# A patch's last 48 rows and the bias: one f32 product against two f16 products on stacked rows

## The reference

```
patches = X cut into 8 x 8 patches of 28 x 28 x 3           # 64 patches of 2352 values, batch 128
tokens  = concat(cls, patches @ W.T + b) * pos_embed        # 65 tokens of 128 values
h = tokens + lstm(layernorm(tokens))                        # 65 steps, state of 128
logits = layernorm(h) @ router_w.T + router_b               # 16 experts, the best 2 of them
out = h + sum over the 2 experts: gate * (gelu(ln @ w1.T + b1) @ w2.T + b2)
```

## Time and profile before

| | |
|---|---|
| time, median of 3 runs | 673.26 us (672.86 to 674.25) |
| the profiled execution | 674.92 us, of it a span of 673.1 us |
| busy, share of the span | PE 92%, PEld 87%, DVE 84%, ACT 73%, POOL 61% |
| mean granted TensorE clock | 0.986 |
| DMA | 141.67 MB, mean 210 GB/s |

### The profile page before, as it was taken

How to read it: one execution, slowest core, us unless ns; L and a number is a source line. 1 busy time by engine, 2 the same in 40 slices (tenths; PEclk the granted TensorE clock), 3 DMA queues, 4 the chain that set the end, 5 groups by cost and what they waited for, 6 DMA issues and landing times.

```text
span 673.1 us, 24553 instructions
## 1 busy us (share of the span) xinstructions
PE 619.0 (92%) x7952; PEld 587.0 (87%) x7952; DVE 562.3 (84%) x1797; ACT 489.7 (73%) x1259; POOL 411.9 (61%) x446
## 2 busy tenths in 40 slices
PE   4899999999999999999998967999999999999970
PEld 4899999999999999999998856788888898888860
DVE  3887888888888888988989878997787887889896
ACT  3687877666677666665665457778888888999883
POOL 0233333477677776667656677777777666666571
PEclk9999999999999999999999989999999999999995
DMA  8987887688888888877876113445554445555675
GB/s 308 384 285 272 267 274 251 235 265 273 267 277 273 265 274 255 247 238 260 263 245 205 52 54 100 112 130 169 165 142 115 120 114 158 156 174 160 188 224 201
DMA packets 71895, 141.67 MB, mean 210 GB/s; under 512 B 13078, under 2 KB 55650, under 8 KB 63838
## 3 DMA queue, kind: packets, MB, share of 16 engines
q1 hardware_dynamic: 62128, 121.69, 58.1%
q0 software_dynamic: 9280, 17.21, 7.3%
q10 hardware_dynamic: 366, 1.21, 0.5%
HBM read 116.35 MB, written 25.66 MB: 211 GB/s over the span
## 4 chain that ended last, share of the span: by engine, by line
PE 57%; DVE 8%; issue 6%; DMA 5%; POOL 3%; ACT 1%; SPq 0%; POOLq 0%; ACTq 0%; DVEq 0%
PE pair L1281 22%; PE pair L1436 11%; PE pair L1454 11%; PE pair L1327 4%; DMA patches<-sent 4%; PE pair L1291 3%; PE pair L1410 2%; DVE patches L1099 2%; PE pair L1296 1%; POOL back L1259 1%; PE pair L1382 1%; DMA field<-back 1%; POOL sent L1235 1%; PE pair L1353 1%; PE pair L1316 1%
## 5 line engine op out<-in xcount | busy, mean ns | idle before, releaser
L1259 POOL DMA_INDIRECT back<-patches x160 | 156.7, 979 | 69.0 <-issue 54.7
L1281 PE MATMUL pair<-field,patches 128*128 128x128 f32 (+1 forms) x1408 | 173.7, 280 | 9.2 <-DMA patches<-in_x 9.2
L1235 POOL DMA_INDIRECT sent<-pay,slot_own x130 | 148.9, 1146 | 40.0 <-issue 37.0
L1281 PEld LDWEIGHTS pair<-field,patches 128*128 128x128 f32 (+1 forms) x1408 | 164.4, 194 | 9.5 <-issue 8.0
L680 ACT ACTIVATE pair<-pair,b1s 128x256 f32<-128x256 f32 x320 | 123.1, 448 | 29.0 <-PE pair L1436 28.3
L605 ACT ACTIVATE gate<-pair,lbias 128x128 f32<-128x128 f32 x260 | 74.1, 367 | 81.4 <-PE pair L1296 79.5
L1247 POOL TENSOR_TENSOR rstd<-veps,cst 128x2 f32<-128x2 f32 (+1 forms) x68 | 57.4, 844 | 94.7 <-DVE veps L800 94.2
L1436 PE MATMUL pair<-patches,ex_hi 128*128 128x256 f16 x640 | 109.8, 274 | 6.0 <-DVE patches L1099 3.7
L1454 PE MATMUL pair<-ex_hi,patches 128*128 x1280 | 111.4, 219 | 2.9 <-DVE patches L1099 1.5
L1099 DVE TENSOR_TENSOR patches<-pair,patches 128x1024 f16<-128x1024 f32 x80 | 97.2, 1215 | 1.7 <-ACT patches L689 1.7
L1281 PE MATMUL pair<-field 128*128 128x128 f16 x1536 | 96.1, 219 | 0.0
(11 more groups left out here) (150 smaller groups left out, 1232.2 us busy)
## 6 DMA issues: line engine op xcount, KB each, us to landing
patches<-in_x SPq DMA_DIRECT2D x62, 1152.0 KB
patches<-sent SPq DMA_DIRECT2D x80, 130.0 KB
field<-in_we SPq DMA_DIRECT2D x64, 128.0 KB
field<-back SPq DMA_DIRECT2D x10, 768.0 KB, 5.2
patches<-in_b SPq DMA_DIRECT2D x80, 64.0 KB
field<-in_pos SPq DMA_DIRECT2D x65, 64.0 KB
out_tower<-h SPq DMA_DIRECT2D x10, 384.0 KB
back<-patches POOLq DMA_INDIRECT x160
```

What stands on the lines that cost most here:

```text
L1235: pool.indirect_dma_start(sent, bass.IndirectOffsetOnAxis(ap=slot_own[:, g % 4, choice, col:col + 1], axis=0), pay[:, t % NP, :], None, bo ...
L1259: pool.indirect_dma_start(back, bass.IndirectOffsetOnAxis(ap=dsti[j % NO][:, k:k + 1], axis=0), yo[j % NO][:, k, :], None, bounds_check=2 ...
L1281: last = pe.matmul(bank_of, l, w_, start=(c == KS and k == 0), stop=(c == KS - 1 and k == 2))
```

## The change: what it does

The rest of a patch moves from the f32 part to the f16 part. Its 48 rows and the row of ones are now loaded twice into one chunk of 128 partitions: rows 0 to 47 and again 64 to 111, with ones in the rows between and behind. The weights of that chunk hold the rounded weights in rows 0 to 63 and their f16 remainders in rows 64 to 127, the bias in row 48 of each half and zeros behind it. One f16 matmul over 128 rows then gives rounded patch times rounded weights plus rounded patch times remainder, and a second one over 64 rows gives patch remainder times rounded weights. The f16 chunks are now the last 8 and the rest, and the f32 chunks the first 10, so the f32 part has one chunk less and the f16 part two matmuls more. ACT's second half of the split grows from 4 chunks to 5, DVE's `xlo` from 8 to 9. SP issues one more load of 48 rows for each patch. On ACT's queue the rest of the weights comes in six small loads, ahead of the 8 chunks that are split. The buffer for position rows has 3 places and not 4.

```diff
-NPOS = 4
+NPOS = 3
 def load_patches(t):
...
-    sp.dma_start(xraw[q][0:KREST, KC, :], x[bass.ds(row + KC * P, KREST), :]
-                 ).then_inc(x_in[q], 16)
+    for first in (0, STACK):
+        sp.dma_start(xraw[q][first:first + KREST, KC, :], x[bass.ds(row + KC * P, KREST), :]
+                     ).then_inc(x_in[q], 16)
...
-act.dma_start(ws[:, 0:KC - KS, :], w[:, KS:KC, :]).then_inc(w_in, 16)
-act.dma_start(ws[0:KBIAS + 1, KC - KS, :], w_rest).then_inc(w_in, 16)
-act.dma_start(ws_raw, w[:, 0:KS, :]).then_inc(ws_in, 16)
+act.dma_start(ws[:, :, :], w[:, 0:NF, :]).then_inc(w_in, 16)
+for first in (0, STACK):
+    act.dma_start(ws_raw[first:first + KREST, KS, :], w_rest[0:KREST, :]).then_inc(ws_in, 16)
+    act.dma_start(ws_raw[first + KREST:first + KREST + 1, KS, :], w_rest[KBIAS:KBIAS + 1, :]
+                  ).then_inc(ws_in, 16)
+    act.dma_start(ws_raw[first + KREST + 1:first + STACK, KS, :], w_rest[KREST:KBIAS - 1, :]
+                  ).then_inc(ws_in, 16)
+act.dma_start(ws_raw[:, 0:KS, :], w[:, NF:KC, :]).then_inc(ws_in, 16)
...
-    split(t, KS // 2, KS).then_inc(hi_done, 1)
+    split(t, KS // 2, KS + 1).then_inc(hi_done, 1)
...
+dve.scalar_tensor_tensor(whi[STACK:P, KS, :], ws_raw[STACK:P, KS, :], W_SCALE, whi[STACK:P, KS, :], ALU.mult,
+                         ALU.subtract)
...
-    dve.tensor_tensor(xlo[r][:, :, :], xraw[q][:, 0:KS, :], xhi[r][:, :, :],
+    dve.tensor_tensor(xlo[r][:, :, :], xraw[q][:, NF:KC + 1, :], xhi[r][:, :, :],
                       ALU.subtract).then_inc(lo_done, 1)
...
 for c in range(a, b):
-    if c < KS:
-        parts = [(l[r][:, c, :], w_[:, c, :]) for l, w_ in ((xhi, whi), (xhi, wlo), (xlo, whi))]
+    s = c - NF
+    if c < NF:
+        parts = [(xraw[q][:, c, :], ws[:, c, :])]
+    elif c < KC:
+        parts = [(l[r][:, s, :], w_[:, s, :]) for l, w_ in ((xhi, whi), (xhi, wlo), (xlo, whi))]
     else:
-        rows = slice(0, P if c < KC else KBIAS + 1)
-        parts = [(xraw[q][rows, c, :], ws[rows, c - KS, :])]
+        parts = [(xhi[r][:, s, :], whi[:, s, :]), (xlo[r][0:STACK, s, :], whi[0:STACK, s, :])]
...
-        project(k, KS, KC + 1)
+        project(k, 0, NF)
...
-    project(t, 0, KS).then_inc(tok_done, 1)
+    project(t, NF, KC + 1).then_inc(tok_done, 1)
```

More of the change, by code:

```diff
@@ L33 @@
 KS = 8
+NF = KC - KS
+STACK = 64
 E, FF = 16, 512
@@ L125, in piece_of_field, with chunks_of_field @@
             return field[:, spent[0] - words:spent[0]]
[L127 to L133, removed]
+        def chunks_of_field(n):
+            return piece_of_field(n * P // 2).bitcast(F16).rearrange("p (a b) -> p a b", a=n)
+        ws = piece_of_field(NF * HID).rearrange("p (a b) -> p a b", b=HID)
+        xhi = [chunks_of_field(KS + 1) for i in range(2)]
+        xlo = [chunks_of_field(KS + 1) for i in range(2)]
+        whi, wlo = chunks_of_field(KS + 1), chunks_of_field(KS)
         posr = piece_of_field(NPOS * HID).rearrange("p (a b) -> p a b", b=HID)
@@ L145, in tower @@
         late = ex_lo[:, E // 2:E, :, :].rearrange("p e m f -> p (e m f)").bitcast(F32)
-        ws_raw = late[:, 0:KS * HID].rearrange("p (a b) -> p a b", a=KS)
-        wih = late[:, KS * HID:(KS + 4) * HID].rearrange("p (a b) -> p a b", a=4)
-        whh = late[:, (KS + 4) * HID:(KS + 8) * HID].rearrange("p (a b) -> p a b", a=4)
+        ws_raw = late[:, 0:(KS + 1) * HID].rearrange("p (a b) -> p a b", a=KS + 1)
+        wih = late[:, (KS + 1) * HID:(KS + 5) * HID].rearrange("p (a b) -> p a b", a=4)
+        whh = late[:, (KS + 5) * HID:(KS + 9) * HID].rearrange("p (a b) -> p a b", a=4)
         b1s = sb("b1s", [P, E * FC])
@@ L315, in tower @@
         N_FIRST, N_WEIGHTS, N_CONST = 2, 4, 3
+        N_STACKED = 7
         R_MASK, R = 12, 16
@@ L449, in load_patches @@
                 if t <= 2:
[L450 removed]
+                    sp.dma_start(xraw[q][:, 0:NF, :], here[:, 0:NF, :]).then_inc(x_in[q], 16)
                 else:
                     sp.dma_start(xraw[q][:, 0:KC, :], here).then_inc(x_in[q], 16)
[L453 to L454 removed]
+                for first in (0, STACK):
+                    sp.dma_start(xraw[q][first:first + KREST, KC, :], x[bass.ds(row + KC * P, KREST), :]
+                                 ).then_inc(x_in[q], 16)
                 if t <= 2:
[L456 removed]
+                    sp.dma_start(xraw[q][:, NF:KC, :], here[:, NF:KC, :]).then_inc(x_head[q], 16)
             sp.wait_ge(ones_in, 1)
@@ L568, in _ @@
             expert_of = act.alloc_register("expert_of")
-            act.dma_start(ws[:, 0:KC - KS, :], w[:, KS:KC, :]).then_inc(w_in, 16)
-            act.dma_start(ws[0:KBIAS + 1, KC - KS, :], w_rest).then_inc(w_in, 16)
-            act.dma_start(ws_raw, w[:, 0:KS, :]).then_inc(ws_in, 16)
+            act.dma_start(ws[:, :, :], w[:, 0:NF, :]).then_inc(w_in, 16)
[6 more added lines that the diff above has]
+            act.dma_start(ws_raw[:, 0:KS, :], w[:, NF:KC, :]).then_inc(ws_in, 16)
             act.wait_ge(setup_dve, 1)
             act.activation(tc[:, 0:1], c2[:, 0:1], ACT.Tanh)
[L576 to L581, removed]
+            act.wait_ge(w_in, 16)
+            act.activation(ws[:, :, :], ws[:, :, :], ACT.Copy, scale=W_SCALE).then_inc(setup_act, 1)
+            act.wait_ge(ws_in, 16 * N_STACKED)
             act.activation(whi[:, :, :], ws_raw, ACT.Copy, scale=W_SCALE).then_inc(setup_act, 1)
@@ L586, in split @@
                 q, r = (t - 1) % NX, (t - 1) % 2
-                return act.activation(xhi[r][:, a:b, :], xraw[q][:, a:b, :], ACT.Copy)
+                return act.activation(xhi[r][:, a:b, :], xraw[q][:, NF + a:NF + b, :], ACT.Copy)
             def recurrent_weights():
@@ L726, in _ @@
             dve.wait_ge(setup_act, 2)
-            dve.scalar_tensor_tensor(wlo[:, :, :].rearrange("p a b -> p (a b)"), ws_raw.rearrange("p a b -> p (a b)"),
-                                     W_SCALE, whi[:, :, :].rearrange("p a b -> p (a b)"), ALU.mult,
+            dve.scalar_tensor_tensor(whi[STACK:P, KS, :], ws_raw[STACK:P, KS, :], W_SCALE, whi[STACK:P, KS, :], ALU.mult,
+                                     ALU.subtract)
+            dve.scalar_tensor_tensor(wlo[:, :, :].rearrange("p a b -> p (a b)"),
+                                     ws_raw[:, 0:KS, :].rearrange("p a b -> p (a b)"),
+                                     W_SCALE, whi[:, 0:KS, :].rearrange("p a b -> p (a b)"), ALU.mult,
                                      ALU.subtract).then_inc(setup_dve, 1)
@@ L1274, in project @@
                 for c in range(a, b):
-                    if c < KS:
-                        parts = [(l[r][:, c, :], w_[:, c, :]) for l, w_ in ((xhi, whi), (xhi, wlo), (xlo, whi))]
-                    else:
-                        rows = slice(0, P if c < KC else KBIAS + 1)
-                        parts = [(xraw[q][rows, c, :], ws[rows, c - KS, :])]
+                    s = c - NF
[3 more added lines that the diff above has]
+                        parts = [(l[r][:, s, :], w_[:, s, :]) for l, w_ in ((xhi, whi), (xhi, wlo), (xlo, whi))]
+                    else:
+                        parts = [(xhi[r][:, s, :], whi[:, s, :]), (xlo[r][0:STACK, s, :], whi[0:STACK, s, :])]
                     for k, (l, w_) in enumerate(parts):
-                        last = pe.matmul(bank_of, l, w_, start=(c == KS and k == 0), stop=(c == KS - 1 and k == 2))
+                        last = pe.matmul(bank_of, l, w_, start=(c == 0), stop=(c == KC and k == 1))
                 return last
```

8 lines of the change are left out of this document (4 added, 4 removed).

## The result

The changed kernel takes 684.8 us, the median of 4 runs (683.52 to 685.81), beside 673.35 us for the kernel before on the same chip. The ratio is 1.0164, with a 95% interval of 1.0143 to 1.0184: 11.4 us slower, where 2.6 us faster was predicted. The profiled execution took 683.52 us with a span of 681.7.

The account below looks back on a forecast made before the run. PE's instructions were taken to bound the steady stage, unless PE is made to wait. Slots at -3.21 us and start at +0.57 gave -2.64, so the median of 673.26 would become 670.6 us, range 669.2 to 671.9.

Parts of the forecast that it names:

- The change on PE: PE's work in a projection slot: two f32 instructions go, two f16 come, 0.116 us less, at most 7.2 over 62 slots.
- the 40 slots that were to keep all 0.116: Slots whose gaps leave PE's whole saving of 0.116 us each: -4.64 us together.
- The tight slots: Slots with short gaps between xn and its transpose on PE: five lose 0.06 us each, others change by nothing.
- 19, at 0.112: Slot 19, one of two where PE already waits and the slot loses 0.112 us; +0.22 for both.
- the six at 0.134: Slots 41, 44, 54, 56, 59, 60: chain runs through DVE's longer L843, 0.134 us lost each, +0.80 together.
- The 0.107 for ACT in slot 57: ACT's second half of the split, grown to 640 columns, stands on the chain once: +0.11 us in the sum.
- -3.09: Forecast change over the slots in us: the sum of -3.21 without slot 0.
- +0.57: At the start: 0.3 us for extra loads and 0.27 for two widened L843 before the first xT_lo.
- (1): PE's whole saving arrives in the slots, 7.2 us less the start: 666.6 to 668 us; chance 0.10.
- (2): Split weights land late behind SP's second patch, delaying what follows by 2 to 3 us: 672.5 to 674; chance 0.13.
- (3): POOL's sends meet DVE's longer L843; 10 to 15 slots lose 0.134 us, +1.3 to 2, so 672.2; chance 0.15.
- (4): PE's clock falls in slots 57 to 61: +4 us or more, 674.8; chance 0.10 with a start beyond 4 us.

Follow-up runs that it names:

- all 128 rows: The changed kernel with its last f16 product over all 128 rows instead of 64, no f16 matmul moved ahead of xn's transpose: 671.61 us, ratio 0.999.
- five ahead: The run with all 128 rows, with five f16 matmuls (the rest's two and one chunk's three) ahead of xn's transpose: 669.95 us, ratio 0.9948.
- the rest's products first: The changed kernel with its two stacked products at the head of the f16 part instead of its end: 683.67 us, ratio 1.015.
- the large load first: The run with five ahead, with the 8 chunks of split weights before the six small loads on ACT's queue: 669.73 us, ratio 0.994.
- two ahead: The run with all 128 rows, with the rest's two f16 products ahead of xn's transpose: 671.99 us, ratio 0.9969.
- three ahead: The kernel before the change, with one chunk's three f16 matmuls ahead of xn's transpose: 673.86 us, ratio 0.9995.

## Why the prediction was wrong

**The step that failed** is the first price in "The change on PE": "The one over 64 rows isn't in the trace; by the same comparison I take it at the full 0.056. Its bounds are 0 and 0.114". It costs 0.056 + 0.25 = 0.31 us in place, more than twice the upper bound. The comparison was between 65 rows and 128, and the experiments put the border between 64 and 65. The prediction had named a dearer 64-row matmul among the signs of being wrong, and had called its ends unlikely for just this comparison. The second fault is in how the bounds were made. They priced an instruction; what changed was the pair of transitions around it, half of them charged to the router product behind. A bound for a shape that is new on PE has to hold the case in which its weight load isn't overlapped, there and back: the row of a 128-row f16 load, some 0.1 us, twice, would have given 0.2 of the 0.25. From slot 1 to 61 the changed kernel differs from the run with all 128 rows by 12.7 us: 53 of 61 slots are 0.21 to 0.25 us longer, 7 are equal (19, 42, 45, 55, 57, 58, 61; other chains end last there) and one is 0.25 shorter. The medians, by 1.0164 against 0.999, differ by 11.7; of the 1.0 between, 0.4 is the start, below.

The Trainium skill's page "TensorE: Matmul & The Clock Gate" (Part 2, Step-by-step: what each phase is for) has PE pull a weight load ahead of running matmuls if their row groups don't conflict or if the load goes to the background weight buffer. The runs agree that this overlap is what is lost, in the rows above, and add when: not with 65 rows, but with 64 and 32. Why PE gives it up at a change of height, whether for a buffer, a group or a switch of the array between two shapes, no run shows. The same page of the Trainium skill (LDWEIGHTS) says that a load of few rows takes as long as one of 128. The trace agrees nearly, 92 ns beside 98, and this duration tells nothing of the cost.

**Right.** 20 f32 instructions take 2.29 us (2.28), the f16 group 1.45 and slots 5.60 once the narrow product is gone, L853 takes 1352 ns (1355), ACT's second half 720 (715). DVE's idle time ahead of the slot's work is then 0.43 us in slot 30 (0.37), and PE's first input gates come at 21.17 us in the changed kernel and at 21.76 with all 128 rows (21.5). PE waits for `xn` in slots 25, 33 and 50 to 53 (with all 128 rows). There is no wait for patches after the start, and the place fewer for positions cost nothing. Of the 40 slots that were to keep all 0.116, 37 kept 0.09 to 0.12; slot 20 kept 0.23, slot 61 lost 0.04, and slot 0 isn't in my count.

**Right in kind, wrong in size.** The tight slots: slots 43 and 50 to 53 were to lose 0.06 and lost 0.11 to 0.12; 17, 25, 33, 42 and 58 were to lose nothing and lost 0.05 to 0.20, while 18, 31 and 48 gained 0.11; 19, at 0.112, lost 0.35; of the six at 0.134, slot 59 lost 0.32 and 41, 56 and 60 between -0.02 and 0.06. The 0.107 for ACT in slot 57 didn't come. Part of the miss is a price that I had left out: where PE waits for `xn`, the transpose's weight load is late as well. With none ahead its row in slot 51 is 0.33 us long, with five ahead 0.28; the kernel before has 0.33 too, in slots 19, 46 and 54, where PE waits. With all 128 rows 14 more slots wait, and 14 times 0.05 is 0.7 us, about what is missing between -3.09 and -2.49. Why slots 19 and 59 lost so much more is open. With -2.49 and a start of +0.79 the traces give -1.7 us; the runs with all 128 rows give ratio 0.999 (0.9968 to 1.0012), and the forecast's 670.6, which is 0.9961, lies just outside that interval. So these two terms were off as well, but it was the narrow product that made the kernel slower.

**The start.** +0.57 was forecast; +0.39 was measured in the changed kernel and +0.79 with all 128 rows. Most of the difference between these two lies in how fast PE ran the second patch's 20 f32 instructions. With all 128 rows they took 4.63 us,

```profile
14.09 4.63 PE L1293 MATMUL pair<-field,patches 128*128 128x128 f32 x20 [1.76 <-DMA patches<-in_x]
```

against 2.50 in the changed kernel, after a wait of similar length (2.07 us). It doesn't follow the rows: the rest's products first, with a 64-row matmul, took 3.86 us there, and the large load first, with all 128 rows, 2.50. Nearly twice the time is what the lower of PE's two levels, 1.2 GHz, would give. The run with two ahead has the same 4.64 us there and shows a granted clock of 0.50 from 14 to 19 us; for the run with all 128 rows that column shows 1.00, so it doesn't settle it. Which level a start gets differs between runs of nearly the same program, and why stays open.

**The rivals.** (1) The whole gain didn't come, for the reason given. (2) The start: the forecast had a late landing of the split weights free up to 13 us. It is free at most up to 11.7: L735, L737 and L853 stand behind them on DVE, ahead of the first `xn`. With the weights at 11.72 DVE comes to L783 at 15.63 without any idle time (15.26 with the large load first, where it waits for `pos`), and at 12.60 the whole 0.87 us is handed on to L783. With them landed by 9.4 the term falls below zero, 28.75 against 28.92. (3) The send beside L853 went from 1.90 to 2.03 us, by the 0.13 that this rival gave it, and POOL's 0.71 of idle time covered it; it cost nothing that shows in the slots where PE is the bound. In slots 49 to 59 no run separates it. (4) The clock's dip stayed behind the projections: in the changed kernel the stretch from 375 to 400 us is at 1.00 and the one from 400 to 425 at 0.86.

**The chances.** They don't add up: the parts that the prediction gives for faster are 0.52, 0.10, 0.04 and 0.05, which is 0.71, and its own figure for faster is 0.68.

## What to carry to other kernels

On PE don't price a new shape by its own duration; look at what stands before and after it. A single f16 matmul over 64 or 32 rows among matmuls over 128 costs 0.21 to 0.25 us more than its 0.056, as much as four full ones; take it over more than 64 rows (65 and 128 were run, with operands that were there anyway), or put narrow ones side by side (two were run). Narrow f32 matmuls, rows other than the first ones, and a step from 64 to 32 rows were not tried. And where PE's saving lies ahead of a wait, move independent matmuls from behind the wait to the front of it: with five ahead that turned 0.999 into 0.9948 here, while three ahead without the saving gave 0.9995.

## What was not expected of the hardware

- The height of a matmul counts at a border between 64 and 65 rows, and only where it changes: 65 rows 0.00 us, 64 and 32 rows 0.25 us with an f32 matmul behind, 64 rows 0.21 with an f16 one, a second narrow one behind the first 0.00 more than a full one.
- The mean duration of an instruction hides this (227 ns and 219), and so does PE's busy share (318.5 of 320 us). The weight load's idle time shows it: 6.6 us for 64 changes to 64 rows, 13.3 for 128.
- A matmul that waits for its operand also pays for its weight load: the transpose of `xn` takes 0.33 us and not 0.28.
